# Copying the turned maxima of the attention: rows taken from VectorE and given to ScalarE, four in a block

## The chip, the cores and the metric

The kernel runs on one core of a Trainium2 chip. A time is the device time of one execution in microseconds; the time before is 1843.28 us, the median of 3 runs from 1840.26 to 1844.48. PE is TensorE (PEld its weight loads), DVE VectorE, ACT ScalarE, POOL GpSimd, SP SyncE.

## The reference, cut to what matters

A tower of two layers on 4 sequences of 513 tokens with 192 channels, in fp32. Two of its stages hold a softmax attention with 12 heads of 16 channels. They have the same form, and the change touches these two alone:

```python
q, k, v = jnp.split(qkv, 3, axis=-1)          # [B, 513, 12, 16] each, turned to [B, 12, 513, 16]
scores = jnp.einsum('bqhd,bkhd->bhqk', q, k) / jnp.sqrt(jnp.float32(Dh))
attn = jax.nn.softmax(scores, axis=-1)
ao = jnp.einsum('bhqk,bkhd->bqhd', attn, v).reshape(B, S, D)
```

Around them stand a tokenizer with sines, a state-space mixer, three MLPs, a mixture of 8 experts and a spiking attention without softmax. None of these is touched.

## The kernel before, in words

`attention` (L1827) does one attention stage. Its work is 12 groups: a batch (4) and a set of 4 heads (3). A group is two pairs of heads, `gi` 0 and 1; a pair has two heads, `e` 0 and 1, one in partitions 0 to 63 and one in 64 to 127. Keys and queries come in 5 tiles of up to 104 rows (`KT`). The stage has two streams that run side by side.

The first stream finds for every query the largest score over all keys, because the exponential needs it. TensorE scores a tile of queries against 512 keys (L1921), VectorE reduces the 104x512 tile to its maximum (L2007); a group has 20 such units, in 10 couples. The 513th key comes from a few small matmuls (L1932) and one maximum (L2018), which also places the maxima in fp16 in the tile `mexp`. TensorE turns them (`turn`, L1943), so that in each of two PSUM banks (one for each `gi`) two single rows of 513 numbers stand, one for each `e`. Each row is then copied into the row of `q2` that the second stream reads as an extra channel of the query (`copy_max`, L1875). The product with the keys, which have -1 there, then carries the subtraction of the maximum by itself.

The second stream does the real scores, transposed: `keys(n)` (L1966) makes two 104x257 score tiles in one of two PSUM pairs, ScalarE takes the exponential of both at once (L2042), and `values(n)` (L1982) multiplies by the values into the one bank `acc`, which ScalarE empties twice a group (`copy_sums`, L2031). A group has 20 exponentials, units `n` in TensorE's loop; a step `t` of it is `keys(2t)`, one couple of the first stream, `keys(2t+1)`, `values(2t-2)`, and now and then the last keys or a turn. The first stream runs 13 couples ahead.

The order is written out by hand, and each engine does its work strictly in it. What ties the engines together:

- `keys(n)` waits until the exponential of unit `n-2` has read the same PSUM pair.
- The first stream's units, the last keys and the two turned banks share three PSUM banks in turn (`ring`, `bank_of`). A unit may be written when what stood three places earlier in the ring has been read. For a turned bank this means both of its rows (`mc_v` and `mc_s`, in `free`).
- `keys` of a group's first two units wait for both rows of their pair.
- ScalarE copies its rows of group `g+1` after the exponential of unit 17 (`NB - 3`) of group `g`; for the first group before its first exponential. VectorE has its copies in the order of the ring.

Of the kernel before, what the change touches and what calls it, by code (L numbers as in the profile page):

```python
# [1826 lines left out]
def attention(c, name, q2, kT, v, aT, att, wts, experts=False):  # L1827
# [12 lines left out]
    with ExitStack() as ctx:  # L1840
# [17 lines left out]
        for n in range(G * PAIRS + 2):  # L1858
            g, u = divmod(n, PAIRS)
# [5 lines left out]
        def bank_of(unit):  # L1865

            return c.bank[place[unit] % 3]

        def copy_max(eng, copy, g, gi, e):

            b, j = groups[g]
            eng.wait_ge(mt, 2 * g + gi + 1)
            bank = bank_of(("max", g, gi)).bitcast(F16)
            r = 64 * e + 32
            copy(q2[r:r + 1, 2 * j + gi, b * T:(b + 1) * T], bank[r:r + 1, 0:T]).then_inc(mc[e], 1)  # L1875

        halves = ExpertHalves(c, ctx) if experts else None
        with nc.Block() as block:
            @block.sync
            def _(sp):  # L1880
                if experts:
                    halves.load(sp)
# [116 lines left out]
            @block.vector  # L1999
            def _(dve):  # L2000
                for unit in ring:
                    if unit[0] == "s":
                        n = unit[1]
                        gi, k, e = S_UNITS[n % NS]
                        qn = KT[k][1]
                        dve.wait_ge(scored, n + 1)
                        dve.reduce_max(mx[0:qn, n // NS % 2, 2 * gi + e, k:k + 1], bank_of(unit)[0:qn, 0:KEYS], X  # L2007
                                       ).then_inc(maxed, 1)
                    elif unit[0] == "last":
                        g = unit[1]  # L2010
                        dve.wait_ge(maxed, NS * (g + 1))
                        dve.wait_ge(lasts, g + 1)
                        if g >= 2:
                            dve.wait_ge(mt, 2 * (g - 1))
                        for x in range(2):
                            a = mx[0:QT, g % 2, :, :].rearrange("p (i e) k -> p i e k", e=2)[:, :, x, :]
                            b_ = bank_of(unit)[0:QT, 0:4 * NK].rearrange("p (i k e) -> p i k e", k=NK, e=2)[:, :, :, x]
                            dve.tensor_tensor(mexp[0:QT, g % 2, :, :, 64 * x + 32], a, b_, ALU.max  # L2018
                                              ).then_inc(placed, 1)
                    else:  # L2020
                        copy_max(dve, dve.tensor_copy, unit[1], unit[2], 0)

            @block.scalar
            def _(act):
                def copy_sums(n):
                    b, j = groups[n // 2]
                    act.wait_ge(summed, NK * (n + 1))
                    if n % 2:
                        act.wait_ge(copied, n)
                    at = b * T + START[n % 2]  # L2030
                    act.copy(aT[:, j, at:at + HALF], acc[:, 0:HALF]).then_inc(copied, 1)  # L2031

                for gi in range(2):
                    copy_max(act, act.copy, 0, gi, 1)
                for n in range(G * NB):
                    g, i = divmod(n, NB)
                    half, k, gi = B_UNITS[i]
                    kn = KT[k][1]
                    act.wait_ge(keyed, 2 * n + 2)
                    if n >= 4:  # L2040
                        act.wait_ge(summed, (n - 4) // 2 + 1)
                    act.activation(p[0:kn, n % 4, :, :],  # L2042
                                   c.pair[2 + n % 2][0:kn, :].rearrange("p (e q) -> p e q", e=2)[:, :, 0:HALF],
                                   ACT.Exp, scale=scale).then_inc(expd, 1)
                    if i == NB - 3 and g + 1 < G:
                        for gi in range(2):
                            copy_max(act, act.copy, g + 1, gi, 1)
                    if i == 1 and g:
                        copy_sums(2 * g - 1)
                    if i == 11:  # L2050
                        copy_sums(2 * g)
                copy_sums(2 * G - 1)
# [1084 lines left out]
```

## Time and profile before

| | |
|---|---|
| median of 3 runs | 1843.28 us |
| the profiled execution | 1847.83 us |
| its span, first to last instruction | 1846.0 us |
| mean granted TensorE clock | 0.847 of full speed |
| first attention stage, first reduce to last exponential | 847.7 to about 1032 us |
| second attention stage, the same | to about 1686 us |
| copies of turned maxima, in both stages | 48 by ScalarE, 48 by VectorE |

The time of the profiled execution is the one against which sums are made, since all durations come from it. Busy shares are means over all stages; the attention stages are read by themselves. Starts are from the begin of the span. Back to back, one instruction of ScalarE or VectorE starts before the record of the one before has ended, so what one costs in a row is the distance of starts and not its duration.

### The profile page before, as it was taken

Reading aid. Unit: us, or ns where it says so; the run is one execution under the profiler, and the core shown is the slowest. Engines: PE = TensorE matmul, PEld = TensorE weight load, DVE = VectorE, ACT = ScalarE, POOL = GpSimd, SP = SyncE. Lnnn points to the kernel's source line nnn. Section 1 sums busy time; section 2 is a strip of 40 time slices with the busy share of each in tenths; the row PEclk is TensorE's granted clock in tenths of the full one; section 3 lists DMA queues with packets and bytes.
Section 4 is the critical chain, followed back from the end, with each engine's and each line's share of the span. In section 5 each row is a group of like instructions: output and inputs, shape, how many; then the busy total and the mean of one; then the engine's idle time right before and its main releaser. Section 6 shows DMA issues by size and latency. Waiting matters only on the chain. (4 is left out here: it accounts for less than half of the span.)

```text
span 1846.0 us, 36517 instructions
## 1 busy us (share of the span) xinstructions
PE 1513.2 (82%) x14190; PEld 1135.7 (62%) x14190; DVE 1306.5 (71%) x2831; ACT 1053.0 (57%) x1872; POOL 411.4 (22%) x428
## 2 busy tenths in 40 slices
PE   5898995877349987899999854998198899999795
PEld 5888985776326675764444544888086554446474
DVE  5988895489646655837999375887365469995666
ACT  6988994433356616444998423665100548896455
POOL 0000000000357711036980013665000320000100
PEclk9999997688555588987999756999598889999898
DMA  5120001000000010002540092121200000000101
GB/s 138 27 65 23 14 2 48 1 4 1 1 7 1 1 33 1 14 1 104 180 131 2 1 271 66 56 62 50 73 1 5 9 2 2 2 2 2 33 1 35
DMA packets 52725, 67.96 MB, mean 37 GB/s; under 512 B 11511, under 2 KB 41465, under 8 KB 52554
## 3 DMA queue, kind: packets, MB, share of 16 engines
q1 hardware_dynamic: 46586, 50.74, 9.0%
q0 software_dynamic: 3840, 9.18, 1.7%
q10 hardware_dynamic: 2128, 5.71, 1.2%
q8 instruction: 114, 1.87, 0.4%
q14 instruction: 57, 0.47, 0.1%
HBM read 46.97 MB, written 18.65 MB: 36 GB/s over the span
## 5 line engine op out<-in xcount | busy, mean ns | idle before, releaser
L2007 DVE TENSOR_REDUCE att_max<-banks 104x1 f32<-104x512 f32 (+1 forms) x480 | 295.9, 682 | 9.7 <-PE banks L1921 5.7
L2042 ACT ACTIVATE att_p<-banks 104x514 f32<-104x514 f32 (+1 forms) x480 | 262.3, 600 | 33.3 <-PE banks L1966 22.6
L339 PE MATMUL banks<-tok_wT,feature_halves 128*128 128x192 f16 x2592 | 229.5, 249 | 22.9 <-DVE feature_halves L365 11.8
L339 PEld LDWEIGHTS banks<-tok_wT,feature_halves 128*128 128x128 f16 x2592 | 217.4, 99 | 31.8 <-DVE feature_halves L365 17.5
L1982 PE MATMUL banks<-att_p,att_v 104*32 104x257 f32 (+1 forms) x1920 | 159.8, 405 | 0.9 <-ACT att_p L2042 0.3
L1966 PE MATMUL banks<-att_q,att_kT 64*104 64x257 f16 (+1 forms) x960 | 155.9, 304 | 2.9 <-ACT att_p L2042 2.5
L1921 PE MATMUL banks<-att_kT,att_q 64*104 64x512 f16 (+1 forms) x480 | 126.3, 424 | 4.9 <-DVE att_max L2007 2.1
L365 DVE TENSOR_TENSOR feature_halves<-features,feature_halves 128x2048 f16<-128x2048 f32 x54 | 123.4, 2285 | 6.1 <-ACT feature_halves L462 6.1
L1966 PEld LDWEIGHTS banks<-att_q,att_kT 64*104 64x104 f16 (+1 forms) x960 | 61.8, 123 | 107.0 <-ACT att_p L2042 80.2
L1146 POOL MEMSET C_start_apart<- 96x5472 f32 x1 | 4.7, 4658 | 476.0 <-POOLq L972 476.0
L462 ACT CAST feature_halves<-features 128x2048 f16<-128x2048 f32 x54 | 102.2, 1893 | 10.8 <-PE banks L339 10.0
L134 PE MATMUL banks<-ones 128*128 128x256 f16 x450 | 59.9, 302 | 56.3 <-PEq L113 27.3
L134 PEld LDWEIGHTS banks<-ones 128*128 128x128 f16 x450 | 48.1, 108 | 67.9 <-issue 53.7
L2761 ACT COPY slot_xT<-banks 128x512 f16<-128x512 f16 x40 | 23.4, 586 | 93.4 <-PE banks L2711 93.4
L2740 PE MATMUL banks<-expert_w,slot_hidden_halves 128*128 128x192 f16 x720 | 65.8, 246 | 12.1 <-DVE slot_hidden_halves L2809 12.1
L2724 PE MATMUL banks<-slot_xT,expert_w 128*128 128x128 f16 x1200 | 75.7, 223 | 0.0
L1819 DVE TENSOR_TENSOR att_qkv_parts<-banks,att_qkv_parts 104x192 f16<-104x192 f32 (+1 forms) x80 | 25.0, 354 | 70.7 <-ACT att_qkv_parts L1799 70.7
L354 DVE SCALAR_TENSOR_TENSOR angle_rest<-raw_T,freq,turns 128x1024 f32<-128x1024 f32 x54 | 69.0, 1278 | 6.2 <-ACT turns L244 5.7
L2699 POOL DMA_INDIRECT expert_out<-slot_y,slot_goes x40 | 61.4, 1536 | 49.1 <-DMA expert_out<-slot_y,slot_goes 38.2
L1758 PE MATMUL banks<-att_qkv_w,xT 96*104 96x384 f32 (+3 forms) x160 | 66.7, 543 | 6.7 <-POOL att_qkv_parts L1734 4.5
L2724 PEld LDWEIGHTS banks<-slot_xT,expert_w 128*128 128x128 f16 x1200 | 72.0, 100 | 0.0
L1921 PEld LDWEIGHTS banks<-att_kT,att_q 64*104 64x104 f16 (+1 forms) x480 | 51.9, 126 | 31.3 <-DVE att_max L2007 19.2
(463 smaller groups left out, 3532.6 us busy)
## 6 DMA issues: line engine op xcount, KB each, us to landing
expert_w_in<-in_L_ffn_w_dram SPq DMA_DIRECT2D x16, 576.0 KB, 4.5
expert_w_halves<-expert_w_halves SPq DMA_DIRECT2D x32, 288.0 KB, 2.5
tok_w<-in_L_tok_W_dram ACTq DMA_DIRECT2D x4, 1152.0 KB, 7.3
expert_w2s<-expert_w_halves SPq DMA_DIRECT2D x1, 4608.0 KB
expert_y<-expert_out SPq DMA_DIRECT2D x6, 513.0 KB
expert_w1s<-expert_w_halves SPq DMA_DIRECT2D x2, 1536.0 KB
raw<-in_x_dram SPq DMA_DIRECT2D x2, 1152.0 KB, 5.7
expert_w1s<-expert_w_halves SPq DMA_DIRECT2D x3, 768.0 KB
```

The source lines that it names most:

```text
L134: pe.matmul(c.bank[7][:, 0:256], ones[:, 0:128], ones, start=True, stop=True)
L339: ins = pe.matmul(c.bank[t // 2][:, (t % 2) * D:(t % 2 + 1) * D], fh[:, s, q, z, t * 128:(t + 1) * 128], wT[:, y, k, 6 * q + wf, :], start ...
L354: own.did(dve.scalar_tensor_tensor(fr[:, n % 2, :], rT[:, k, hf * HALF:(hf + 1) * HALF], freq_col(k, f), fm[:, n % 2, :], ALU.mult, ALU.su ...
L365: dve.tensor_tensor(fh[:, s, :, 1, :], feat[:, s, :, :], fh[:, s, :, 0, :], ALU.subtract).then_inc(flow, 1)
L462: act.copy(fh[:, s, :, 0, :], feat[:, s, :, :]).then_inc(fhigh, 1)
L1758: ins = pe.matmul(c.bank[n % 2][0:m, 0:2 * D], c.xT[0:r, o, at:at + m], w[0:r, o, 0:2 * D], start=(o == 0), stop=(o == 1))
L1921: pe.matmul(bank_of(("s", n))[0:qn, 0:KEYS], q2[r, 2 * j + gi, b * T + q0:b * T + q0 + qn], kT[r, 2 * j + gi, b * T:b * T + KEYS], start=T ...
L1966: pe.matmul(c.pair[2 + n % 2][0:kn, 512 * e:512 * e + HALF], kT[r, 2 * j + gi, b * T + k0:b * T + k0 + kn], q2[r, 2 * j + gi, b * T + STAR ...
L1982: ins = pe.matmul(acc[32 * hh:32 * hh + 32, 0:HALF], v[0:kn, b, k, h, :], p[0:kn, (n + hh // 2) % 4, hh % 2, :], start=(k == 0), stop=(k = ...
L2007: dve.reduce_max(mx[0:qn, n // NS % 2, 2 * gi + e, k:k + 1], bank_of(unit)[0:qn, 0:KEYS], X).then_inc(maxed, 1)
L2042: act.activation(p[0:kn, n % 4, :, :], c.pair[2 + n % 2][0:kn, :].rearrange("p (e q) -> p e q", e=2)[:, :, 0:HALF], ACT.Exp, scale=scale). ...
L2724: ins = pe.matmul(ps, ws[:, s, at:at + 128], xt[:, s, b, :], start=(k == 0), stop=(k == len(TERMS) - 1))
```

## The change

VectorE copies no turned row any more. ScalarE copies both rows of both pairs, four in one block, at the places where it copied two. The semaphore that counts the rows of `e` = 0 is still counted, now by ScalarE; the waits of TensorE are word for word the same.

```diff
@@ vector
                             dve.tensor_tensor(mexp[0:QT, g % 2, :, :, 64 * x + 32], a, b_, ALU.max
                                               ).then_inc(placed, 1)
-                    else:
-                        copy_max(dve, dve.tensor_copy, unit[1], unit[2], 0)
@@ scalar
-                for gi in range(2):
-                    copy_max(act, act.copy, 0, gi, 1)
+                def copy_maxima(g):
+                    for gi in range(2):
+                        for e in range(2):
+                            copy_max(act, act.copy, g, gi, e)
+
+                copy_maxima(0)
                 for n in range(G * NB):
...
                     if i == NB - 3 and g + 1 < G:
-                        for gi in range(2):
-                            copy_max(act, act.copy, g + 1, gi, 1)
+                        copy_maxima(g + 1)
```

ScalarE in the middle of the first attention stage, before (att_p are exponentials, att_q the rows of maxima, att_aT the sums):

```order
L2042 ACTIVATE att_p<-banks 104x514 x6
L1875 COPY att_q<-banks 1x513 x2
L2042 ACTIVATE att_p<-banks 97x514 x2
L2042 ACTIVATE att_p<-banks 104x514 x2
L2031 COPY att_aT<-banks 128x257
```

and now, with line numbers of the changed file:

```order
L2044 ACTIVATE att_p<-banks 104x514 x6
L1875 COPY att_q<-banks 1x513 x4
L2044 ACTIVATE att_p<-banks 97x514 x2
L2044 ACTIVATE att_p<-banks 104x514 x2
L2029 COPY att_aT<-banks 128x257
```

Two copies more stand between the exponentials of units 17 and 18. VectorE in the same stage, before (att_max are the reduces, att_max_placed the maxima with the last key):

```order
L2018 TENSOR_TENSOR att_max_placed<-att_max,banks 104x10 x2
L2007 TENSOR_REDUCE att_max<-banks 104x1 x4
L1875 COPY att_q<-banks 1x513 x2
L2007 TENSOR_REDUCE att_max<-banks 104x1 x4
L2007 TENSOR_REDUCE att_max<-banks 97x1 x2
```

and now:

```order
L2018 TENSOR_TENSOR att_max_placed<-att_max,banks 104x10 x2
L2007 TENSOR_REDUCE att_max<-banks 104x1 x8
L2007 TENSOR_REDUCE att_max<-banks 97x1 x2
```

The reduces close up. TensorE, GpSimd and SyncE have the same instructions in the same order as before.

## Rows read from the trace of the kernel before

**Rows 1.** Page, costliest groups: line engine op, out<-in xcount | busy, mean ns | idle before, releaser.

```profile
L2007 DVE TENSOR_REDUCE att_max<-banks 104x1 f32<-104x512 f32 (+1 forms) x480 | 295.9, 682 | 9.7 <-PE banks L1921 5.7
L2042 ACT ACTIVATE att_p<-banks 104x514 f32<-104x514 f32 (+1 forms) x480 | 262.3, 600 | 33.3 <-PE banks L1966 22.6
```

**Rows 2.** Busy time by stretch: start:end length, busy us (x count) of each engine.

```profile
core 0: us, PE busy (x) PEld busy (x) DVE busy (x) ACT busy (x) POOL busy (x), PEclk, DMA share, GB/s
946.00:959.70 13.70, 13.65 (x164) 6.47 (x162) 13.38 (x25) 12.39 (x24) 13.39 (x7) 1.00 0.39 130
```

**Rows 3.** Timeline, ScalarE, two blocks of copies: start, length, [idle before <-releaser].

```profile
945.27 0.59 ACT L2042 ACTIVATE att_p<-banks 104x514 f32<-104x514 f32 x1
946.02 1.07 ACT L1875 COPY att_q<-banks 1x513 f16<-1x513 f16 x2 [0.15 <-PE banks L1943]
946.51 0.58 ACT L1875 COPY att_q<-banks 1x513 f16<-1x513 f16 x1
947.11 1.09 ACT L2042 ACTIVATE att_p<-banks 97x514 f32<-97x514 f32 x2
957.32 2.25 ACT L2042 ACTIVATE att_p<-banks 104x514 f32<-104x514 f32 x4 [0.68 <-PE banks L1966]
959.72 1.06 ACT L1875 COPY att_q<-banks 1x513 f16<-1x513 f16 x2
```

**Rows 4.** Timeline, TensorE and VectorE around the first of these blocks.

```profile
945.58 0.63 PE L1943 MATMUL banks<-att_ident,att_max_placed 104*128 104x104 f16 x10
946.32 0.76 DVE L1875 COPY att_q<-banks 1x513 f16<-1x513 f16 x2
946.79 0.12 PEld L1921 LDWEIGHTS banks<-att_kT,att_q 64*104 64x104 f16 x1 [0.33 <-DVE att_q L1875]
947.10 1.29 DVE L2007 TENSOR_REDUCE att_max<-banks 104x1 f32<-104x512 f32 x2
947.25 0.64 PE L1982 MATMUL banks<-att_p,att_v 104*32 104x257 f32 x8
947.85 0.32 PE L1966 MATMUL banks<-att_q,att_kT 64*104 64x257 f16 x2
947.71 1.40 DVE L2007 TENSOR_REDUCE att_max<-banks 104x1 f32<-104x512 f32 x2
```

**Rows 5.** Instructions by line and shape, the copies.

```profile
L1875 ACT COPY att_q<-banks 1x513 f16<-1x513 f16 x48 | 25.6, 579 | 35.0 <-PE banks L1943 34.4
L1875 DVE COPY att_q<-banks 1x513 f16<-1x513 f16 x48 | 18.1, 415 | 5.4 <-PE banks L1943 4.7
```

**Rows 6.** Timeline, start of the first stage: copies, table load, steps at half and full clock.

```profile
862.34 1.11 ACT L1875 COPY att_q<-banks 1x513 f16<-1x513 f16 x2 [15.51 <-PE banks L1943]
863.47 1.28 ACT L2042 ACT_TABLE_LOAD   x1
865.42 0.46 PE L1966 MATMUL banks<-att_q,att_kT 64*104 64x257 f16 x2 [0.21 <-ACT att_p L2042]
867.46 0.46 PE L1966 MATMUL banks<-att_q,att_kT 64*104 64x257 f16 x2
869.32 0.31 PE L1966 MATMUL banks<-att_q,att_kT 64*104 64x257 f16 x2
870.46 0.31 PE L1966 MATMUL banks<-att_q,att_kT 64*97 64x257 f16 x2
```

**Rows 7.** Busy time by stretch: experts, end of each attention stage (columns as in rows 2).

```profile
1220.00:1292.00 72.00, 63.30 (x916) 60.42 (x916) 55.67 (x90) 42.33 (x89) 43.73 (x34) 1.00 0.19 54
1019.00:1034.00 15.00, 14.25 (x108) 3.87 (x105) 0.00 (x0) 9.75 (x19) 0.04 (x1) 0.51 0.00 1
1673.00:1688.00 15.00, 12.61 (x136) 4.74 (x133) 0.00 (x0) 12.90 (x26) 0.44 (x1) 1.00 0.00 1
```

**Rows 8.** Timeline, ScalarE, last copies of maxima and last copy of sums, both stages.

```profile
1014.66 1.06 ACT L1875 COPY att_q<-banks 1x513 f16<-1x513 f16 x2 [0.28 <-PE banks L1943]
1033.33 0.37 ACT L2031 COPY att_aT<-banks 128x257 f32<-128x257 f32 x1 [1.20 <-PE banks L1982]
1672.06 1.06 ACT L1875 COPY att_q<-banks 1x513 f16<-1x513 f16 x2 [0.28 <-PE banks L1943]
1686.92 0.37 ACT L2031 COPY att_aT<-banks 128x257 f32<-128x257 f32 x1 [0.76 <-PE banks L1982]
```

## The prediction, made before the changed kernel ran

> **What bounds the kernel now.** I read the page's costliest groups first, then the busy times of one group of attention, then the timeline of ScalarE, and last that of TensorE and VectorE beside it.
>
> The page puts the reduces of VectorE at the top, 295.9 us, ahead of the exponentials with 262.3 us [rows 1]. The busy times say the same of one group, 13.70 us long: VectorE 13.38, ScalarE 12.39 [rows 2]. From these two views alone VectorE looks like the engine to relieve, and ScalarE like one with 1.31 us a group to spare. The reader should not stop there, because a busy share does not say whether a stall lies on the loop that sets the pace.
>
> The timeline of ScalarE shows the pace. Its copies of maxima start at 946.02 and again at 959.72, so a group takes 13.70 us, and its idle time is in known places: one hole of 0.68 before unit 14, where TensorE does the last keys first, and small gaps between couples of exponentials [rows 3]. Around the copies there is none: copies at 946.02 and 946.51, the exponential of unit 18 at 947.11 [rows 3]. TensorE's next pair of key matmuls that matters, `keys(20)`, needs unit 18's exponential to have left its PSUM pair. That exponential starts at 947.11 and takes about 0.60 [rows 1], so it ends at 947.71, and `keys(20)` starts at 947.85, 0.14 later. The value matmuls before it ended at 947.89 by the modelled record, so TensorE was free for it at almost the same moment [rows 4]. So at this place ScalarE's last exponential is what comes last, TensorE had nothing to spare beyond a few hundredths, and everything after it (ScalarE's unit 20, VectorE's next couple) hangs on `keys(20)` and the score couple behind it.
>
> VectorE at the same place: it copies from 946.32, starts the next reduce at 947.10 and the one after at 947.71 [rows 4]. The reduce after that belongs to the couple that TensorE issues behind `keys(20)`. The last row of the group shows it: two reduces from 947.71 take 1.40, though one is 0.68 and two in a row start about 0.60 apart (compare the 1.29 of the two from 947.10). So the second began about 1.40 - 0.69 = 0.71 after the first, 0.11 later than it could: VectorE waited there for TensorE.
>
> **The change part by part.** There are 12 blocks of copies in each attention stage: one before the first exponential, 11 in the loop (group 11 has no successor). That is 22 in the loop and 2 at the starts.
>
> Removed from VectorE: 48 copies, 0.38 us each (0.76 for two in a row) [rows 4], 18.1 us by duration [rows 5]. I cost this at nothing. What it wins ends at the first reduce of the couple behind `keys(20)`, for which VectorE waits already, and which comes later now. Between, VectorE can start the next reduce at about 946.83 and not 947.10; it then only waits longer.
>
> Added to ScalarE: two copies in each of 22 blocks in the loop. In a row they start 0.49 apart (946.02 to 946.51) [rows 3], so the exponential of unit 18 starts 2 x 0.49 = 0.98 us later, at 948.09, and ends at 948.69. `keys(20)` follows at 948.83. The whole 0.98 is on the loop: from there on the next group runs as before, since every engine takes its start from `keys(20)`. Nothing gives it back later, because the hole before unit 14 is TensorE's own order and the couples are at the pace of TensorE and VectorE. 22 x 0.98 = 21.6 us. Bounds: above, the duration in place of the distance, 2 x 0.58 = 1.16, gives 25.5 us. Below, if VectorE came out of the block with a lead, the couples that it now paces could run at the shortest seen, 1.14 apart at full clock (869.32 to 870.46 [rows 6]), rather than 2 x 0.60 = 1.20. With 5 such couples a group that is 0.3 us back, 22 x 0.3 = 6.6, so 15 us. I take 21.6, since the reduce behind `keys(20)` is late and not early.
>
> Waits moved. A turned bank is free after its second row. The first bank was free when VectorE's first copy ended, 946.32 + 0.42 = 946.74; TensorE waited 0.33 for it and loaded at 946.79 [rows 4]. Now it is ScalarE's second copy, 946.51 + 0.58 = 947.09, so about 0.35 later. Behind that wait in TensorE's order are `keys(19)` and `values(16)`, which then end near 948.24 rather than 947.89. That is ahead of `keys(20)` at 948.83, so it costs nothing; if the exponentials did not wait too, it would be 22 x 0.35 = 7.7 us. The second bank is free after the fourth copy, 946.02 + 3 x 0.49 + 0.58 = 948.07, also ahead of 948.83, and its score stands behind `keys(20)` in the order.
>
> The two blocks at the starts. Before: copies at 862.34, the table load at 863.47, key matmuls of the next step at 865.42 when the first exponential is out [rows 6]. Two copies more delay the load by about 0.95. TensorE is at the low clock, 1.2 GHz, there: steps take 2.04 (865.42 to 867.46) and 1.86, and 1.14 once the clock is at 2.4 GHz from about 869 [rows 6]. If the clock rises at the same moment, a step fewer is done slow, and of 0.95 some 0.5 is left: 867.46 becomes 868.40, then one third of a step slow and two thirds fast, 0.67 + 0.77, gives 869.84 in place of 869.32. Bounds 0 and 1.0 each; I take 0.5, in sum 1.0 us.
>
> The sum: 21.6 + 1.0 = 22.6 us. On the profiled execution's own 1847.83 that makes 1870.4. It stands 4.55 above the median, so for the median I forecast 1843.3 + 22.6 = 1866 us, 1.2% slower.
>
> One rule speaks for the change. A copy of one row takes ScalarE 579 ns and VectorE 415 [rows 5], so here the engine that takes the rows over is the slower by 164 ns. The Trainium skill ("VectorE: DVE Perf Modes", Specifications) says that VectorE sits closer to SBUF and ScalarE closer to PSUM. By that a row out of PSUM would be at least no dearer on ScalarE: at VectorE's 0.38 in a row the loop would lose 22 x 0.76 = 16.7 us and not 21.6. The row decides against it.
>
> **The rivals.**
>
> VectorE sets the pace. For it: its 13.38 of 13.70 [rows 2]. Then 0.76 less a group would make the group 12.94 us, 24 x 0.76 = 18 us faster, 1825 us. Against it: it waited 0.11 behind `keys(20)`, and ScalarE could not take 2 more copies without losing its own place. Chance 0.05.
>
> ScalarE's idle time swallows the copies. For it: 1.31 us a group are idle [rows 2], more than the 0.98 added; the time would be 1843, no change. Against it: 0.68 of it is the hole that TensorE's order makes, the rest lies in small gaps before other units, and with two PSUM pairs ScalarE can't work ahead to use them. Chance 0.04.
>
> The clock falls inside attention. TensorE stood idle for hardly 0.05 of 13.70 a group [rows 2]. Now it has about 0.35 more at the first bank and 0.6 before `keys(20)`, in one place. Against a fall: among the experts the clock held 2.4 GHz with TensorE busy 63.3 of 72, 88% [rows 7], and here it would be 13.65 of 14.68, 93%. For it: at the end of the first stage, where the first stream has run out, the clock was 1.2 GHz though TensorE was busy 95% by the record, and at the end of the second it was not [rows 7]. So the edge is near when work thins out. A step at 1.2 GHz takes 2.04 in place of 1.20; of a slow stretch of 20 us some 8 us are lost. One in each stage gives 1866 + 16 = 1882 us, more if they repeat. Chance 0.10.
> The Trainium skill ("TensorE: Matmul & The Clock Gate", A second HAM failure mode: psum-queue depth-cycling) tells of a kernel whose short pauses of TensorE between groups of matmuls made the clock go up and down. By that page each block could cost a slow stretch. The 0.33 wait at the same place does not do it in this trace.
>
> Small things of either sign stay within the forecast: the end of a stage takes 18.67 us at 1.2 GHz (1014.66 to 1033.33) and 14.86 at 2.4 (1672.06 to 1686.92) [rows 8], so if the change shifts which end falls into a slow stretch, the time moves by 3.8 us, with what follows perhaps 6.
>
> **How the numbers follow.** Forecast 0.81: 1866 us, its own range 1857 to 1873. VectorE sets the pace 0.05, idle time swallows it 0.04, clock 0.10. The range for 8 in 10 is 1857 to 1876: it takes in the 15 us of the lower bound (1858), the 25.5 plus 2 of the upper (1871) and most of the shifts of the clock, and leaves out the rest of the clock rival. 0.2% is 3.7 us, about what a measurement of this kernel can tell from no change. Faster: 0.05 of VectorE and 0.01 for a lucky clock with little lost, 0.06. Same: 0.04. Slower: 0.90.
>
> **What would show it right or wrong.** In the profile of the changed kernel: 96 copies of L1875 on ScalarE, none on VectorE; blocks of four, 2.05 long; from one block to the next 14.68 us in place of 13.70; no idle time of ScalarE between the block and unit 18, and TensorE waiting some 0.5 us for the exponential before `keys(20)`; VectorE busy about 12.6 of 14.7. If the distance of blocks is below 14.3, VectorE's lead was worth something; above 15.0, the banks or the clock cost more than I say. A distance at or below 13.7 makes the forecast wrong. If the granted clock shows 1.2 GHz in the middle of a stage, it is the clock rival.

## The result and the profile after

The changed kernel takes 1898.74 us, median of 4 runs from 1894.37 to 1904.59, beside 1843.83 for the kernel before in the same series: ratio 1.030, 95% interval 1.027 to 1.034. I had forecast 1866 and a range of 1857 to 1876. The direction was right, and the 22.6 us that I forecast are less than half of the 55. The profiled execution, whose rows are read below, spans 1894.6 us beside 1846.0, which is 48.6 us more.

The reduces and the exponentials (groups as in [rows 1]) and the copies (as in [rows 5]) of the changed kernel; the exponential's line L2042 is now L2044:

```profile
L2007 DVE TENSOR_REDUCE att_max<-banks 104x1 f32<-104x512 f32 (+1 forms) x480 | 299.2, 682 | 71.7 <-PE banks L1921 68.7
L2044 ACT ACTIVATE att_p<-banks 104x514 f32<-104x514 f32 (+1 forms) x480 | 264.3, 599 | 49.3 <-PE banks L1966 39.3
L1875 ACT COPY att_q<-banks 1x513 f16<-1x513 f16 x96 | 55.6, 579 | 36.8 <-PE banks L1943 34.0
```

All 96 copies are on ScalarE, each as long as before (579 ns). VectorE has not become free for anything: the idle time before its reduces rose from 9.7 us [rows 1] to 71.7, nearly all of it waiting for TensorE's scores.

ScalarE from block to block, the answer to [rows 3]; the row at 958.68 is the second copy of the block at 958.07 alone:

```profile
958.07 2.40 ACT L1875 COPY att_q<-banks 1x513 f16<-1x513 f16 x4 [0.15 <-PE banks L1943]
...
958.68 0.58 ACT L1875 COPY att_q<-banks 1x513 f16<-1x513 f16 x1
...
960.49 2.18 ACT L2044 ACTIVATE att_p<-banks 97x514 f32<-97x514 f32 x4
...
973.10 2.40 ACT L1875 COPY att_q<-banks 1x513 f16<-1x513 f16 x4
...
990.79 2.40 ACT L1875 COPY att_q<-banks 1x513 f16<-1x513 f16 x4
```

The copies start 0.61 apart (958.07 to 958.68), where the two of before started 0.49 apart. Unit 18 starts 2.42 after the first copy and not 1.09. That is 1.33 us more a block, and the blocks lie 15.03 apart (958.07 to 973.10), just 1.33 more than the 13.70 of before. So the whole lengthening of the block is on the loop, as forecast, but the term itself is 1.33 and not 0.98.

TensorE and VectorE around the same block, the answer to [rows 4]:

```profile
958.39 0.42 PE L1921 MATMUL banks<-att_kT,att_q 64*104 64x512 f16 x1
958.85 0.69 DVE L2007 TENSOR_REDUCE att_max<-banks 104x1 f32<-104x512 f32 x1 [0.51 <-PE banks L1921]
959.37 0.12 PEld L1921 LDWEIGHTS banks<-att_kT,att_q 64*104 64x104 f16 x1 [0.86 <-ACT att_q L1875]
959.40 0.39 PE L1921 MATMUL banks<-att_kT,att_q 64*104 64x512 f16 x1 [0.59 <-ACT att_q L1875]
959.83 0.69 DVE L2007 TENSOR_REDUCE att_max<-banks 104x1 f32<-104x512 f32 x1 [0.29 <-PE banks L1921]
961.21 0.15 PEld L1966 LDWEIGHTS banks<-att_q,att_kT 64*104 64x104 f16 x2 [1.22 <-issue]
961.24 0.31 PE L1966 MATMUL banks<-att_q,att_kT 64*104 64x257 f16 x2 [0.77 <-ACT att_p L2044]
961.79 2.60 DVE L2007 TENSOR_REDUCE att_max<-banks 104x1 f32<-104x512 f32 x4 [1.27 <-PE banks L1921]
```

TensorE has two holes: 0.59 (0.86 between weight loads) before the score that waits for the first turned bank, and 0.77 before `keys(20)`, where it waits for unit 18's exponential. VectorE stands 1.27 us before the couple behind `keys(20)`: what it was relieved of is idle time there.

The second loss is in the clock. Busy time by stretch (columns as in [rows 2]), first stage of the changed kernel:

```profile
880.50:887.40 6.90, 6.65 (x46) 2.47 (x48) 3.87 (x6) 4.56 (x9) 6.75 (x4) 0.51 0.50 171
887.40:928.30 40.90, 37.06 (x436) 17.43 (x432) 34.45 (x60) 36.76 (x71) 39.98 (x19) 1.00 0.55 175
...
1023.90:1030.70 6.80, 6.68 (x46) 2.49 (x48) 3.86 (x6) 4.45 (x9) 0.00 (x0) 0.50 0.02 4
```

The clock is at 1.2 GHz in four stretches of 6.8 us in the middle of this stage (from 880.5, 928.3, 976.1 and 1023.9; three more in the second stage), each beginning in the hole before `keys(20)`. In the kernel before, the clock was 1.00 all through the middle of both stages; [rows 2] show one group of it. The last of the four comes with a DMA share of 0.02, the first with 0.50, so the transfers are not what they have in common. The `keys` of two steps in such a stretch:

```profile
880.75 0.45 PE L1966 MATMUL banks<-att_q,att_kT 64*104 64x257 f16 x2 [0.77 <-ACT att_p L2044]
882.79 0.46 PE L1966 MATMUL banks<-att_q,att_kT 64*104 64x257 f16 x2
```

A step takes 2.04 (880.75 to 882.79) there, in place of 1.20. From one block to the next such a group is 17.69 us long (973.10 to 990.79) in place of 15.03.

Stage by stage, from the first reduce to the last exponential, the changed kernel's profile is 27.2 and 27.0 us longer than before's. Four parts make up the 54.2: 22 blocks in the loop of 1.33 more, 29.3 us; 7 slow groups of some 2.65 more, 18.6; the end of the second stage, where the clock fell and had held before, 3.7; and both starts, 2.8. The rest of the kernel, which the change does not touch, was 5.6 us shorter in this execution than in the profiled one of before. In all eleven profiles that rest varies by 10 us.

### The profile page after: what moved, and what is told of

Its sections match the earlier page's. It is cut to its first block and busy times, and to the rows that moved or that the text cites. A ratio compares the mean times of both kernels' runs of the same rounds, so it can differ in the third digit from the quotient of the medians.

```text
span 1894.6 us, 36517 instructions
## 1 busy us (share of the span) xinstructions
PE 1543.6 (81%) x14190; PEld 1140.6 (60%) x14190; DVE 1289.3 (68%) x2783; ACT 1086.0 (57%) x1920; POOL 411.1 (22%) x428
## 5 line engine op out<-in xcount | busy, mean ns | idle before, releaser
L2007 DVE TENSOR_REDUCE att_max<-banks 104x1 f32<-104x512 f32 (+1 forms) x480 | 299.2, 682 | 71.7 <-PE banks L1921 68.7
L2044 ACT ACTIVATE att_p<-banks 104x514 f32<-104x514 f32 (+1 forms) x480 | 264.3, 599 | 49.3 <-PE banks L1966 39.3
L1966 PE MATMUL banks<-att_q,att_kT 64*104 64x257 f16 (+1 forms) x960 | 162.2, 323 | 21.9 <-ACT att_p L2044 21.9
L1982 PE MATMUL banks<-att_p,att_v 104*32 104x257 f32 (+1 forms) x1920 | 173.5, 436 | 0.3
L1921 PE MATMUL banks<-att_kT,att_q 64*104 64x512 f16 (+1 forms) x480 | 131.3, 448 | 17.3 <-ACT att_q L1875 12.9
L1982 PEld LDWEIGHTS banks<-att_p,att_v 104*32 104x32 f32 (+1 forms) x1920 | 40.9, 114 | 60.6 <-issue 51.1
L1875 ACT COPY att_q<-banks 1x513 f16<-1x513 f16 x96 | 55.6, 579 | 36.8 <-PE banks L1943 34.0
```

Of the source, the lines that this page charges most:

```text
L1921: pe.matmul(bank_of(("s", n))[0:qn, 0:KEYS], q2[r, 2 * j + gi, b * T + q0:b * T + q0 + qn], kT[r, 2 * j + gi, b * T:b * T + KEYS], start=T ...
L1966: pe.matmul(c.pair[2 + n % 2][0:kn, 512 * e:512 * e + HALF], kT[r, 2 * j + gi, b * T + k0:b * T + k0 + kn], q2[r, 2 * j + gi, b * T + STAR ...
L1982: ins = pe.matmul(acc[32 * hh:32 * hh + 32, 0:HALF], v[0:kn, b, k, h, :], p[0:kn, (n + hh // 2) % 4, hh % 2, :], start=(k == 0), stop=(k = ...
L2044: act.activation(p[0:kn, n % 4, :, :], c.pair[2 + n % 2][0:kn, :].rearrange("p (e q) -> p e q", e=2)[:, :, 0:HALF], ACT.Exp, scale=scale). ...
```

## The experiments

**The order of the copies.** What makes a copy cost 0.61?

```diff
-                    for gi in range(2):
-                        for e in range(2):
+                    for e in range(2):
+                        for gi in range(2):
                             copy_max(act, act.copy, g, gi, e)
```

> The changed kernel with the four copies of a block in the other order: both rows of partition 32 first, then both of partition 96. In the profile of the changed kernel the copies of a block start 0.605 us apart, and not 0.49 as the two of before. Theory A (a start partition other than that of the instruction before costs about 0.115 us): the distances become 0.49, 0.605, 0.49, and 0.61 to the exponential; the block takes 2.19 in place of 2.42, blocks lie 14.80 us apart at full clock in place of 15.03. Theory B (the two new copies are dearer by themselves, for instance through the second semaphore or the row at partition 32): 0.605 stays between all or most of them, 15.03. The pause before keys(20) is 0.23 shorter by A; if the falls of the clock come from the pause, there are as many as in the changed kernel (7 within the stages) or fewer.

ScalarE in one block: the first two copies, the third, and unit 18; then TensorE at the first turned bank.

```profile
957.89 1.06 ACT L1875 COPY att_q<-banks 1x513 f16<-1x513 f16 x2 [0.15 <-PE banks L1943]
958.98 0.58 ACT L1875 COPY att_q<-banks 1x513 f16<-1x513 f16 x1
960.07 0.60 ACT L2044 ACTIVATE att_p<-banks 97x514 f32<-97x514 f32 x1
959.70 0.39 PE L1921 MATMUL banks<-att_kT,att_q 64*104 64x512 f16 x1 [1.07 <-ACT att_q L1875]
```

The first two copies together last 1.06, so they start 0.48 apart; the third starts at 958.98, 0.60 after the second, and unit 18 at 960.07, 2.18 after the first copy in place of 2.42. Theory A held in every distance, and blocks lie 14.79 apart at full clock where it said 14.80. The time did not follow: 1900.38 us, ratio 1.030 (1.027 to 1.033), as with the changed kernel. The clock fell more often, in shorter stretches: 7 of 3.4 to 6.8 us in the middle of the first stage and 7 in the second, for instance (busy times, columns as in [rows 2])

```profile
883.10:886.50 3.40, 3.40 (x27) 1.04 (x24) 2.19 (x4) 2.82 (x6) 3.40 (x2) 0.50 0.19 73
```

I had expected as many falls or fewer. A block 0.24 shorter did not save the clock. The expectation also overlooked where TensorE waits in this order: the first bank is now free only after the third copy, so the whole hole, 1.07 us, stands before its score, and none is left before `keys(20)`.

**One semaphore for all rows.** The rival for the 0.61 was the second semaphore.

```diff
-            copy(q2[r:r + 1, 2 * j + gi, b * T:(b + 1) * T], bank[r:r + 1, 0:T]).then_inc(mc[e], 1)
+            copy(q2[r:r + 1, 2 * j + gi, b * T:(b + 1) * T], bank[r:r + 1, 0:T]).then_inc(mc_s, 1)
...
-                        for e in range(2):
-                            pe.wait_ge(mc[e], 2 * g + gi + 1)
+                        pe.wait_ge(mc_s, 2 * (2 * g + gi + 1))
```

The wait for a turned bank in `free` is changed in the same way.

> The changed kernel, but all four copies count one semaphore, in the changed kernel's order (32, 96, 32, 96). Theory A (start partition): copies 0.605 apart as in the changed kernel, blocks 15.03 us apart at full clock. Theory B (another semaphore than the instruction before costs the 0.115): 0.49 apart, blocks about 14.65 apart.

Timeline of ScalarE in one block, and in the last row its second copy alone:

```profile
959.25 2.40 ACT L1875 COPY att_q<-banks 1x513 f16<-1x513 f16 x4 [0.15 <-PE banks L1942]
961.67 0.60 ACT L2042 ACTIVATE att_p<-banks 97x514 f32<-97x514 f32 x1
959.86 0.58 ACT L1875 COPY att_q<-banks 1x513 f16<-1x513 f16 x1
```

Still 0.61 (959.25 to 959.86), block 2.42. The semaphore is out. With both runs: two copies of the same start partition start 0.49 apart, of another 0.605. In the first experiment the pairs at one partition lie in different banks and are still cheap, and in the changed kernel the dear ones lie in the same bank and in different ones, so the bank is not the cause either. The time was 1900.58 us, ratio 1.030 (1.028 to 1.032). The clock fell 4 times in the middle of the first stage, as in the changed kernel, and 7 times for 3.4 us each in the second, where the changed kernel had 3 falls of 6.8.

The Trainium skill ("ScalarE: Activation LUTs", What ACT_TABLE_LOAD costs) says that back-to-back ACTIVATEs overlap by about 93 ns. The trace agrees for copies at one partition, 579 - 490 = 89 ns, and differs where the start partition changes: 579 - 605 leaves no overlap at all.

**Three rows on ScalarE, one on VectorE.**

```diff
+                    for gi, e in ((0, 1), (1, 0), (1, 1)):
+                        copy_max(act, act.copy, g, gi, e)
...
+                    elif unit[2] == 0:
+                        copy_max(dve, dve.tensor_copy, unit[1], 0, 0)
```

TensorE's waits for the rows are counted to match.

> ScalarE copies three rows of a block (pair 0 upper, pair 1 lower, pair 1 upper), VectorE one (pair 0 lower). If a block's length on ScalarE is the whole price: copies at 0, 0.605, 1.21, exponential at 1.82, that is 0.73 longer than before's 1.09, blocks 14.43 us apart at full clock. If VectorE's unloading had a worth of its own, or the banks a price, it lies off the line between 13.70 (two rows) and 15.03 (four). The pause before keys(20) is some 0.6 shorter than with four rows: falls of the clock between 0 and 7.

Timeline of ScalarE, two blocks, and of TensorE before `keys(20)`:

```profile
967.53 1.79 ACT L1875 COPY att_q<-banks 1x513 f16<-1x513 f16 x3
969.35 1.09 ACT L2048 ACTIVATE att_p<-banks 97x514 f32<-97x514 f32 x2
981.96 1.79 ACT L1875 COPY att_q<-banks 1x513 f16<-1x513 f16 x3
970.09 0.32 PE L1969 MATMUL banks<-att_q,att_kT 64*104 64x257 f16 x2 [0.69 <-ACT att_p L2048]
```

Unit 18 starts 1.82 after the first copy, and the blocks lie 14.43 apart (967.53 to 981.96), both to the hundredth as expected. The price of a block is its length on ScalarE, and the rows taken off VectorE are worth nothing. There is no stretch at 1.2 GHz in the middle of either stage (busy times of the first, columns as in [rows 2]):

```profile
880.00:1029.00 149.00, 139.87 (x1638) 64.90 (x1638) 129.68 (x229) 134.95 (x259) 82.02 (x39) 1.00 0.30 95
```

The time was 1870.52, beside 1845.54 before, ratio 1.014 (1.012 to 1.016). Of its 25 us, 22 x 0.73 = 16 are the loop; at the end of both stages the clock fell, in the second one where it had held before (3.4 us more), and the start of the first stage stayed slow for longer, 18.18 us from first exponential to that of the next group where before had 14.88.

**Idle matmuls in both holes.** Does the pause of TensorE bring the clock down?

```diff
+                def busy(times):
+                    ones = c.ones[:, :].bitcast(F16)
+                    for _ in range(times):
+                        pe.matmul(acc[:, 264:512], ones[:, 0:128], ones[:, 0:248], start=False, stop=False,
+                                  skip_group_check=True)
+
                 def keys(n):
                     g, i = divmod(n, NB)
+                    if g and i == 0:
+                        busy(7)
...
+                        if n >= (LEAD + 9) * 2 and n % NS == 5:
+                            busy(4)
                         free(("s", n))
```

> The changed kernel, with idle matmuls (248 columns, 128 by 128, into unused columns of the accumulator's bank) where TensorE pauses: 4 before the first score that waits for a turned bank, 7 before keys(20). Theory C (the clock falls because of the pause at the blocks): no stretch at 1.2 GHz within a stage between its start and its last group; blocks 15.03 us apart in all groups, so 7 slow groups of some 2.5 us are gone, 17 us, and the time is about 1880. Rival D (the falls come from elsewhere, such as the transfers or the shift of the stage against other work): the slow groups stay, the time stays at about 1898. If the idle matmuls are in the way, blocks lie further apart than 15.03.

TensorE before `keys(20)`, and then busy times: first stage, its end, second stage (columns as in [rows 2]):

```profile
955.21 0.64 PE L1992 MATMUL banks<-att_p,att_v 104*32 104x257 f32 x8
955.78 0.92 PE L1959 MATMUL banks<-ones 128*128 128x248 f16 x7
956.63 0.32 PE L1976 MATMUL banks<-att_q,att_kT 64*104 64x257 f16 x2
```

```profile
880.00:1028.00 148.00, 147.12 (x1687) 71.82 (x1686) 124.02 (x215) 133.80 (x257) 80.37 (x38) 1.00 0.29 92
1028.50:1044.00 15.50, 13.51 (x147) 5.25 (x143) 0.00 (x0) 14.65 (x28) 0.00 (x0) 1.00 0.01 2
1540.00:1693.00 153.00, 152.02 (x1741) 74.13 (x1739) 127.59 (x222) 138.14 (x264) 0.00 (x0) 1.00 0.01 2
```

The clock is 1.00 to the end of both stages, and the blocks lie 15.04 apart in all groups, and 15.03 without them, so the idle matmuls cost next to nothing. 1874.67 us (1870.36 to 1880.47) beside 1845.54, ratio 1.017 (1.015 to 1.019). The 29 us that are left happen to be the copies' 22 x 1.33 = 29.3. Stage by stage it is less even: from first to last exponential the stages are 12.1 and 15.5 us longer than before's, which is 14.6 of copies each, 0.9 each for a slower start, and 3.4 less in the first stage, whose end now runs fast. So of the 26 us between this run and the changed kernel some 22 are what the changed kernel had lost by its clock, and 3.4 are a slow end that the kernel before had too. Rival D fell, and theory C held: matmuls that nobody reads, put into the holes, took all 7 falls away. They are of 128 by 128, larger than those of the attention around them, and none was put anywhere else in the loop. So it is not shown that they must stand in the holes.

**Idle matmuls before keys(20) only.** The same kernel without those in the first hole; the edit is shown against the run before it:

```diff
-                        if n >= (LEAD + 9) * 2 and n % NS == 5:
-                            busy(4)
```

> The changed kernel with the 7 idle matmuls before keys(20) alone; the pause before the score that waits for the first turned bank stays. If the pause before keys(20), where TensorE stands idle 0.8 us and more, is what the clock falls for, no slow groups are left, as with both filled (blocks 15.03, about 1875). If the two pauses count together, some slow groups come back, between 0 and 7.

TensorE at the first turned bank, and the busy times of the middle and the end of the first stage:

```profile
953.79 0.39 PE L1921 MATMUL banks<-att_kT,att_q 64*104 64x512 f16 x1 [0.59 <-ACT att_q L1875]
880.00:1033.00 153.00, 145.84 (x1692) 70.84 (x1690) 123.27 (x214) 138.33 (x267) 79.63 (x37) 1.00 0.27 87
1034.00:1047.00 13.00, 13.00 (x102) 3.54 (x100) 0.00 (x0) 8.76 (x17) 0.00 (x0) 0.50 0.01 1
```

No slow groups in the middle, nor in the second stage, with the first hole left open at 0.59: filling the one before `keys(20)` is enough. The end of the first stage was slow again (last row), which is 3.3 us, and the time was 1879.83, ratio 1.018 (1.016 to 1.020).

**The kernel before with two idle copies in each block.** My 0.98 by itself, with VectorE and the banks as before: the added copies go from a constant tile to a scratch tile.

```diff
                         for gi in range(2):
                             copy_max(act, act.copy, g + 1, gi, 1)
+                        for gi in range(2):
+                            act.copy(spare[96:97, gi, 0:T], idle[96:97, gi, 0:T])
```

> The kernel before, with two copies more on ScalarE at the end of each block in the loop: one row at partition 96, from a constant tile to a scratch tile, which nobody reads. VectorE keeps its copies and the banks come free as before, so this is ScalarE's time alone, without a change of start partition among the copies. Theory A (each costs its 0.49 and the whole stands on the loop, start partition the reason for the rest): unit 18 is 0.98 late, blocks 14.68 us apart at full clock, the figure of my forecast. Theory B (a copy more costs 0.605 whatever its partition): 14.91. If the banks or VectorE matter, the distance is below 14.68 by what they were worth. If a pause of 0.98 at keys(20) is enough for the clock, there are slow groups; at three rows (0.73) there were none, at four (1.33) 7.

ScalarE in a block, TensorE's `keys(20)` at another, and busy times (columns as in [rows 2]) of a stretch at 1.2 GHz:

```profile
1000.56 1.06 ACT L1877 COPY att_q<-banks 1x513 f16<-1x513 f16 x2 [0.16 <-PE banks L1945]
1001.53 1.13 ACT L2051 COPY att_spare<-consts 1x513 f16<-1x513 f16 x2
1002.67 1.70 ACT L2044 ACTIVATE att_p<-banks 97x514 f32<-97x514 f32 x3
956.39 0.31 PE L1968 MATMUL banks<-att_q,att_kT 64*104 64x257 f16 x2 [0.99 <-ACT att_p L2044]
```

```profile
1018.80:1025.70 6.90, 6.90 (x52) 2.19 (x50) 4.55 (x8) 4.71 (x9) 0.00 (x0) 0.51 0.01 4
```

Unit 18 starts 2.11 after the first copy (1000.56 to 1002.67), 1.02 later than before; groups at full clock took 14.73 us, where A had 14.68. So two copies of one start partition cost 1.03, and the term of my forecast was right for those within 0.05. But the time was 1893.98 us beside 1846.95, ratio 1.026 (1.023 to 1.028): 47 us for an addition of 22 x 1.03 = 23. The clock fell 5 times in the middle of the first stage and 6 in the second. Even with the copies at the price I gave, the forecast would have missed half of the loss. TensorE has one hole here, 0.99 before `keys(20)`, and none at the first bank.

**The opposite change: all four rows on VectorE.**

```diff
-                        copy_max(dve, dve.tensor_copy, unit[1], unit[2], 0)
+                        for e in range(2):
+                            copy_max(dve, dve.tensor_copy, unit[1], unit[2], e)
...
-                for gi in range(2):
-                    copy_max(act, act.copy, 0, gi, 1)
...
-                    if i == NB - 3 and g + 1 < G:
-                        for gi in range(2):
-                            copy_max(act, act.copy, g + 1, gi, 1)
```

> The opposite change: VectorE copies all four rows in a block in the order of the ring, ScalarE none. ScalarE wins 1.09 us a group, VectorE does two copies more. Theory A (both engines and TensorE are near the pace, so either direction loses): TensorE waits 0.35 to 0.5 more for the first bank, keys(19) and values(16) slip, VectorE becomes the pace at 13.38 + 0.7 to 0.9: blocks 14.0 to 14.3 us apart, time 1852 to 1859. Rival (only ScalarE's block was on the loop): blocks below 13.70, time below 1843.

Timeline around a block of VectorE:

```profile
949.89 1.81 DVE L1875 COPY att_q<-banks 1x513 f16<-1x513 f16 x4
950.89 0.12 PEld L1921 LDWEIGHTS banks<-att_kT,att_q 64*104 64x104 f16 x1 [0.86 <-DVE att_q L1875]
951.46 0.60 ACT L2041 ACTIVATE att_p<-banks 97x514 f32<-97x514 f32 x1 [0.76 <-PE banks L1966]
...
964.38 1.80 DVE L1875 COPY att_q<-banks 1x513 f16<-1x513 f16 x4
```

Blocks 14.49 apart, a little beyond the 14.0 to 14.3 expected, because VectorE's copies too stand further apart in this order: 1.81 for four in a row of alternating partition, of which the last takes 0.43, is (1.81 - 0.43) / 3 = 0.46 each, beside 0.76 - 0.41 = 0.35 for two of one partition [rows 4]. The time was 1856.27, ratio 1.005 (1.003 to 1.007). Now VectorE's copies are on the loop and ScalarE waits, 0.76 before the exponential behind the block. Before is faster than a shift in either direction. Blocks 0.79 longer would be 22 x 0.79 = 17 us; in the profile 3.2 of them come back at the end of the first stage, where the clock held, and 5.3 in the rest of the kernel, which varies from run to run. The clock held in the middle too, although TensorE's matmuls wait 0.59 for the first bank here, as they do in the changed kernel.

**Idle matmuls for the kernel before.** Is there a version that beats both?

```diff
                 for s in range(LEAD):
                     score_pair(s)
+                    if s < LEAD - 1:
+                        busy(c.bank[7][:, 0:256], 2)
...
                         score_pair(LEAD + t)
+                        if LEAD + t > G * PAIRS + 1:
+                            busy(bank_of(("last", G - 1))[:, 0:256], 2)
                         keys(2 * t + 1)
```

> A version that may beat both: the kernel before, with idle matmuls of 256 columns where TensorE has little to do and the clock was at 1.2 GHz: two after each score couple ahead of the first exponential, and two in each step after the first stream has ended. Expected, if activity there keeps 2.4 GHz: the first steps of each stage take 1.2 us in place of 2.04 (2.5 to 3.3 us a stage), the end of the first stage 14.9 in place of 18.7 us (3.8, and some 2 in what follows): 8 to 12 us faster, about 1834. Rival: the clock stays low there, and the idle matmuls cost 1 to 4 us.

Busy time of the start of the first stage:

```profile
850.00:873.90 23.90, 23.52 (x113) 9.27 (x112) 21.16 (x37) 6.96 (x11) 21.12 (x10) 0.50 0.44 153
```

No change: 1846.70 beside 1846.95, ratio 0.999 (0.998 to 1.001). At the start of the first stage the clock stayed at 1.2 GHz for 24 us with the idle matmuls, and the first exponential came 18.4 us after the first reduce in place of 17.1, so they were in the way. So the start was left alone, and one matmul a step kept at the end:

```diff
                         score_pair(LEAD + t)
+                        if LEAD + t > G * PAIRS + 1:
+                            busy(bank_of(("last", G - 1))[:, 0:256], 1)
                         keys(2 * t + 1)
```

> The kernel before with one idle matmul of 256 columns in each step after the first stream has ended, and none at the start: the version with two, and two after each early score couple, measured no change, with its first exponential 2.7 us late in the first stage and its tails 13.1 us long in both stages, where before has 14.7 and 11.3. If one idle matmul a step keeps the clock at 2.4 GHz and costs nothing, both tails take about 11.5 us: the first stage wins 3 us and the heads after it up to 2, so 1842 beside 1847, or 0.2% faster. Rival: one is too little for the clock, and the time is before's.

Last copies of maxima and last copy of sums, as in [rows 8], of both stages, and the busy time of the first stage's end:

```profile
1012.33 1.06 ACT L1875 COPY att_q<-banks 1x513 f16<-1x513 f16 x2 [0.28 <-PE banks L1943]
1027.91 0.37 ACT L2038 COPY att_aT<-banks 128x257 f32<-128x257 f32 x1 [0.76 <-PE banks L1987]
1662.72 1.06 ACT L1875 COPY att_q<-banks 1x513 f16<-1x513 f16 x2 [0.28 <-PE banks L1943]
1678.31 0.37 ACT L2038 COPY att_aT<-banks 128x257 f32<-128x257 f32 x1 [0.76 <-PE banks L1987]
```

```profile
1009.00:1027.00 18.00, 17.42 (x190) 7.28 (x187) 1.53 (x5) 15.74 (x31) 0.00 (x0) 1.00 0.01 2
```

1840.02 us beside 1844.25, ratio 0.997 (0.996 to 0.999). It is the fastest of all, by about 0.3%. The end of the first stage takes 15.58 us in place of 18.67 [rows 8]; that of the second 15.59 in place of 14.86, so the matmul is not free where the clock would have held anyway. These two make 2.4 of the 4.2 us; the rest was not taken apart.

## Why the prediction was right and wrong

**The pace, right.** Everything stood on unit 18's exponential and `keys(20)` behind it. Two, three and four rows on ScalarE give distances of 13.70, 14.43 and 15.03 us with blocks of 1.09, 1.82 and 2.42: the differences are the same, 0.73 and 1.33.

**VectorE's gain at nothing, right.** Its 48 copies went, and its idle time before the reduces rose by 62 us. The three-row run lies on the line without any credit for VectorE.

**The two turned banks, right.** The first bank was 0.5 later than before rather than 0.35, since the second copy starts 0.61 after the first; in time it was still hidden before `keys(20)`. But the 0.59 that TensorE's matmuls now wait there is idle time that before did not have.

**The added copies: the term was mis-sized.** "2 x 0.49 = 0.98" took the distance from the only pair in the trace, which was of one start partition. In the new order each copy has another start partition than the one before it. The rows held the other distance too: the exponential at 947.11, which starts at partition 0, stands 0.60 behind the copy at 946.51, which starts at 96 [rows 3]. The term is 1.33 a block, 29.3 us for 22, beyond my upper bound of 25.5. That bound took the duration of 0.58 for the most that a copy could cost. Each of the two new ones costs 0.605, and between the two old ones 0.49 became 0.605 as well: 1.21 + 0.12 = 1.33. The sign that I gave, a distance of blocks above 15.0, came out at 15.03, and it was neither the banks nor the clock, as I had said it would be, but the copies. The clock's groups are those at 17.7.

**The clock: the step that failed.** I gave the fall inside a stage a chance of 0.10, because the experts held 2.4 GHz with TensorE busy 88% and the group would be at 93%. That compared mean busy shares, and the mean did not decide it: in the middle of the stage TensorE was busy over 90% between the falls (37.06 of 40.90 us), and the clock fell all the same. The runs show that the idle time of TensorE around the blocks is what it fell with. It came as 7 short stretches, where I had priced one long one a stage. The 7 slow groups and the slower end of the second stage make 18.6 + 3.7 = 22 us, and my sum had nothing for them.

What TensorE did around a block at full clock, and how often the clock fell in the middle of the two stages together:

| run | hole before the first bank's score, us | hole before `keys(20)`, us | falls |
|---|---|---|---|
| before | below 0.05 | below 0.05 | 0 |
| four rows, both holes filled | below 0.1 | below 0.1 | 0 |
| four rows, the second hole filled | 0.59 | below 0.1 | 0 |
| four rows on VectorE | 0.59 | below 0.1 | 0 |
| three rows | below 0.1 | 0.69 | 0 |
| before with idle copies | below 0.1 | 0.99 | 11 |
| four rows, other order | 1.07 | below 0.1 | 14 |
| four rows, one semaphore | 0.50 | 0.83 | 11 |
| four rows, the changed kernel | 0.59 | 0.77 | 7 |

So the hole before `keys(20)` is not the cause by itself: three rows have 0.69 of it and no fall, and the other order has none of it and the most falls. The sum of the holes and the longest of them put these runs in the same two classes, and no run tells which of the two counts. The number of falls, from one profile each, rises with the longest hole, 7 at 0.77 and 14 at 1.07. But the 7 are the longer ones, and in their time at 1.2 GHz the four runs are close, 48 to 55 us. The experts, my comparison, differ in another way as well, since their matmuls (L2740, L2724) are of 128 by 128. Whether that is why they held the clock at 88% was not tested.

The Trainium skill ("TensorE: Matmul & The Clock Gate", A second HAM failure mode: psum-queue depth-cycling) tells of this for another kernel: short pauses between groups of matmuls, often enough, made the clock go up and down. The trace agrees: here it went down in every third group. I had named the page and given the rival 0.10.

**The starts, mis-sized.** I had 1.0 us for both, and they took 2.8. From the first reduce to the first exponential it is 18.4 us in place of 17.1 in both stages, so the two copies more cost 1.29 there and not 0.95. From there to unit 18 of the first group the first stage lost 0.76 beyond the block's 1.33, with the low clock until 6.1 us after the first exponential in place of 4.3, and the second stage won 0.49. They were not tested alone.

In sum, of the forecast's two terms the copies cost 29.3 in place of 21.6 and the starts 2.8 in place of 1.0, and the clock took 22 that the sum did not have. These are 54 of the 55 us between the medians. That they meet so closely is in part luck, since the untouched rest of the kernel alone varies by more than that between executions.

What stays open: how much idle time the clock bears, and in what form, and why the same kernel's falls last 6.8 us in one stage and 3.4 in the other with one semaphore. The forecast's direction and its account of the loop were right by their mechanism and not by luck.

## What to carry to other kernels

Before work is moved to the engine with the lower busy share, look where in its order it lands: here, behind an exponential that TensorE waits for with two buffers, all of it counted, and the relief elsewhere was worth nothing. A price read from neighbours in the trace holds only for the same neighbours: check partition and order as well as shape. And ask of every added wait of TensorE in a loop that runs at full clock what happens to the clock; one run with idle matmuls in the hole tells it apart from the wait itself.

## What the runs showed of the hardware

Copies of one row on ScalarE start 0.49 us apart if they have the same start partition, and 0.605 if not, whatever their bank or semaphore; on VectorE the figures are 0.35 and about 0.46, where the semaphore changed together with the partition. The partitions tried were 32 and 96. Idle time of TensorE of 1.0 to 1.4 us once in 15 us, in one hole or in two, was enough to bring its clock to 1.2 GHz for stretches of 3.4 to 6.8 us, 7 to 14 times in the two stages, though it was busy over 90% of the time between them; with 0.6 and 0.7 us of it there was no fall. Seven idle matmuls of 248 columns before `keys(20)` kept it at 2.4 GHz without making a block longer.
